# Attention on one core: VectorE sums four tiles of probabilities in one operation, and TensorE's 32-column sets go from six in four blocks to five in three

## The chip, the cores and the metric

The kernel runs on one core of one Trainium2 chip. The metric is the device time of one execution, in microseconds (us).

## What is computed

A gated cross-attention block and a gated feed-forward block. The part that matters here is the attention over 4 batches and 16 heads, with 1024 queries, 2048 keys and 32 columns a head:

```python
attn = jnp.einsum('bhqd,bhkd->bhqk', q, k) * scale
attn = jnp.clip(attn, -CLAMP, CLAMP)
attn = jax.nn.softmax(attn, axis=-1)
x = jnp.einsum('bhqk,bhkd->bqhd', attn, v).reshape(B, Nq, Cq)
```

Around it stand the projections of the queries, keys and values, the output projection, and the feed-forward network, which the change does not touch.

## The kernel before

The stages follow one another: `project_queries`, `project_keys_values`, `attend`, `project_out`, `feed_forward`. Only `attend` is changed.

**Units and steps.** A unit is one half of one head: 512 queries against all 2048 keys. There are 128 units. Each goes through four steps. In a step TensorE computes two different things in turn:

- `scores` (L683): for 128 queries of the unit that is being scored, one 512-key quarter into each of the PSUM banks 0 to 3. Quarters 0 and 1 are half 0, quarters 2 and 3 are half 1. VectorE reduces each half (128x1024) to one maximum a row, `maxima` (L868). The next step's scores of a half wait for this step's maximum of that half (`max_done`), since they overwrite its banks.
- `keys` (L702): for the unit whose maxima are known, the scores once more, transposed (128 keys by 512 queries), with the negated maximum folded in as two extra rows. ScalarE takes the exponential (`exps`, L806) into `probT`, sixteen tiles of 128x512 a unit. Three PSUM banks rotate under these, so a `keys` matmul waits for an earlier exponential.

The lags in the line `TURN, KEYS, PV, SUMS, FOLD = 5, 6, (9, 10), 11, 12` say how many steps behind its scoring a unit comes to each piece of work. I call a step by its number modulo 4: step 3 is the last of a unit's scoring. After its two maxima VectorE does `split_maxima`, five tiny reductions that combine and split the row maxima, at the end of step 3.

**What is summed.** A unit's 32-column work on TensorE goes to the four 32-partition groups of PSUM bank 7, one matmul a group; four (or three) such matmuls are a set. Four sets are the probabilities times the values (`values`, L741), two blocks of two sets. ScalarE copies bank 7 to `partial` (L827), and TensorE adds the four groups with `fold` (L752). The softmax denominators need the sum of all sixteen tiles. GpSimd adds the first twelve into `gp_sum` (L627, L632), and the column sums are matmuls with a tile of ones: tiles 12, 13 and 14 in `fold_values` (L754), tile 15 and the two halves of `gp_sum` in `last_sums` (L765). ScalarE then copies the result out of bank 7 (`gather`, L837).

**The order on TensorE in a step** is written out by hand: scores 0, keys 0, scores 1, keys 1, then whichever of `values`, `fold_values`, `last_sums` and `turn_maxima` (L723, which transposes the negated maxima; ScalarE copies them to `q_stack`, L818) belongs there, then scores 2, keys 2, scores 3, keys 3. Before the change there is one block in each step: `last_sums` in step 0, `values` and `turn_maxima` in step 1, `values` in step 2, `fold_values` in step 3.

VectorE's order in a step is maximum of half 0, maximum of half 1, and `split_maxima` in step 3. Every engine runs its own program in order; semaphores join them. A loop body holds 24 steps, six units.

## Time and profile before

| what | before |
|---|---|
| time, median of 3 runs | 3306.59 us (3306.49 to 3313.1) |
| the profiled execution's own time | 3304.32 us |
| its span | 3302.5 us |
| TensorE busy over the span | 3096.9 us (94%) |
| VectorE, ScalarE, GpSimd busy | 1998.2 (61%), 1558.6 (47%), 1911.2 (58%) us |
| mean granted TensorE clock | 0.969 |

The span is cut into stages by the first and last instruction of each. The attention stage runs from the first scores at 478.38 us to the last `gather` at 2344.47 us, more than half of the whole. In it the pattern of one unit repeats, so what one unit takes, times the number of units, is the stage.

### The profile page before, as it was taken

The page shows a single profiled execution, that of the slowest core. Times are in us where ns is not written, and L with a number is a line of the kernel's source. Part 1 is how long each engine was busy: PE and PEld are TensorE (multiplying, and loading weights), DVE is VectorE, ACT ScalarE, POOL GpSimd, SP SyncE. Part 2 cuts the span into 40 slices and gives each one's busy share as a digit, 9 for nine tenths or more (in the row PEclk, how much of TensorE's full clock was granted, in tenths as well). Part 3 has the DMA queues.
Part 4 walks back from the last instruction along what each step waited for, and adds up shares of the span by engine and source line. Part 5 has one row for each costly group of instructions (what it writes and reads, how often), then busy time and mean ns, then how long its engine had stood idle before and what let it go on. Part 6 is the DMA issues. An engine that isn't in the chain of part 4 may idle for free. (4 is left out here: it accounts for less than half of the span.)

```text
span 3302.5 us, 51612 instructions
## 1 busy us (share of the span) xinstructions
PE 3096.9 (94%) x15941; PEld 1905.8 (58%) x15941; DVE 1998.2 (61%) x2788; ACT 1558.6 (47%) x2847; POOL 1911.2 (58%) x897
## 2 busy tenths in 40 slices
PE   6799979999999999999999999999564999999999
PEld 5588854444444444444444444444243788888887
DVE  8766657666766666676666667666387333333332
ACT  2222217766766777676677667677321211111111
POOL 4655538888888888888888888888453100000000
PEclk9899979999999999999999999999777999999999
DMA  4556672222221222222122222211485000000000
GB/s 165 203 193 216 213 246 63 59 58 58 58 55 47 52 58 58 58 58 53 47 54 58 58 58 58 54 46 38 147 256 166 1 26 26 26 26 26 26 13 13
DMA packets 142094, 263.25 MB, mean 80 GB/s; under 512 B 16960, under 2 KB 57920, under 8 KB 134720
## 3 DMA queue, kind: packets, MB, share of 16 engines
q1 hardware_dynamic: 141344, 253.82, 27.1%
q10 hardware_dynamic: 672, 8.39, 0.8%
q8 instruction: 49, 0.80, 0.1%
q14 instruction: 29, 0.24, 0.0%
HBM read 168.84 MB, written 93.32 MB: 79 GB/s over the span
## 5 line engine op out<-in xcount | busy, mean ns | idle before, releaser
L868 DVE TENSOR_REDUCE at_half_max<-ps 128x1 f32<-128x1024 f32 x1024 | 1210.0, 1221 | 555.1 <-PE ps L683 548.2
L632 POOL TENSOR_TENSOR at_gp_sum<-at_gp_sum,at_probT 128x1024 f32<-128x1024 f32 x512 | 1218.6, 2380 | 42.1
L806 ACT ACTIVATE at_probT<-ps 128x512 f32<-128x512 f32 x2048 | 1071.1, 601 | 159.8 <-PE ps L702 139.0
L683 PE MATMUL ps<-at_k_stack,at_q_stack 96*128 96x512 f32 x2048 | 877.3, 430 | 27.2 <-DMA at_k_stack<-kT_hi 17.8
L702 PE MATMUL ps<-at_q_stack,at_k_stack 98*128 98x512 f32 x2048 | 808.2, 396 | 1.4 <-ACT at_probT L806 1.1
L683 PEld LDWEIGHTS ps<-at_k_stack,at_q_stack 96*128 96x128 f32 x2048 | 389.8, 191 | 465.5 <-DVE at_half_max L868 383.2
L741 PE MATMUL ps<-at_probT,at_v_head 128*32 128x512 f32 x4096 | 492.5, 598 | 0.9 <-ACT at_probT L806 0.9
L627 POOL TENSOR_TENSOR at_gp_sum<-at_probT 128x1024 f32<-128x1024 f32 x128 | 304.2, 2377 | 316.4 <-ACT at_probT L806 316.4
L702 PEld LDWEIGHTS ps<-at_q_stack,at_k_stack 98*128 98x128 f32 x2048 | 390.2, 191 | 70.1 <-ACT at_probT L806 7.1
L1392 POOL TENSOR_TENSOR ff_x_in<-ff_x_in,ff_b_half 128x2048 f32<-128x2048 f32 x8 | 36.8, 4604 | 601.5 <-DVE ff_x_in L1414 601.5
L1377 ACT ACTIVATE ff_y<-ps,ff_b_t 128x512 f32<-128x512 f32 x128 | 88.2, 689 | 612.9 <-PE ps L1340 612.9
L1431 DVE CAST ff_y_hi<-ff_y 128x512 fp32r<-128x512 f32 x128 | 61.5, 481 | 483.8 <-PE ps L1355 476.9
L741 PEld LDWEIGHTS ps<-at_probT,at_v_head 128*32 128x32 f32 x4096 | 106.8, 109 | 246.5 <-issue 197.6
L1340 PE MATMUL ps<-ff_h_hi,w_hi 128*128 128x512 f32 x512 | 202.8, 396 | 5.7 <-DVE ff_h_lo L1423 5.7
L1355 PE MATMUL ps<-w_hi,ff_y_hi 128*128 128x512 f32 x512 | 204.4, 399 | 0.0
L1340 PE MATMUL ps<-ff_h_hi,w_lo 128*128 128x512 f32 x512 | 202.7, 396 | 0.0
L1340 PE MATMUL ps<-ff_h_lo,w_hi 128*128 128x512 f32 x512 | 202.6, 396 | 0.0
L1355 PE MATMUL ps<-w_hi,ff_y_lo 128*128 128x512 f32 x512 | 201.5, 393 | 0.0
L1355 PE MATMUL ps<-w_lo,ff_y_hi 128*128 128x512 f32 x512 | 201.4, 393 | 0.0
L818 ACT ACTIVATE at_q_stack<-ps 2x512 fp32r<-2x512 f32 x128 | 75.0, 586 | 244.7 <-PE ps L723 244.7
L82 POOL TENSOR_TENSOR kv_square<-kv_k_hi 128x512 f32<-128x512 f32 x64 | 77.0, 1203 | 129.0 <-ACT kv_k_hi L453 124.5
L827 ACT COPY at_partial<-ps 128x512 f32<-128x512 f32 x128 | 75.1, 587 | 146.3 <-PE ps L741 146.3
(154 smaller groups left out, 3867.9 us busy)
## 6 DMA issues: line engine op xcount, KB each, us to landing
at_k_stack<-kT_hi SPq DMA_DIRECT2D x128, 256.0 KB, 4.9
kT_hi<-kv_k_hi SPq DMA_DIRECT2D x16, 1024.0 KB, 4.2
kT_lo<-kv_k_lo SPq DMA_DIRECT2D x16, 1024.0 KB, 6.5
v_heads<-kv_v_out SPq DMA_DIRECT2D x16, 1024.0 KB, 5.7
at_q_stack<-qT_hi SPq DMA_DIRECT2D x128, 128.0 KB, 3.3
at_k_stack<-kT_lo SPq DMA_DIRECT2D x64, 256.0 KB, 4.3
at_v_head<-v_heads SPq DMA_DIRECT2D x64, 256.0 KB, 5.1
kv_c_in<-in_ctx_dram SPq DMA_DIRECT2D x16, 768.0 KB, 7.2
```

The lines of the kernel that those rows point to most:

```text
L82: pool.tensor_tensor(square[:, :], tile, tile, ALU.mult).then_inc(bound_done, 1)
L627: pool.tensor_tensor(gp_sum[lane % 2][:, :, :], pairs[:, 0:2, :], pairs[:, 2:4, :], ALU.add) \
L632: pool.tensor_tensor(gp_sum[lane % 2][:, :, :], gp_sum[lane % 2][:, :, :], pairs[:, 2 * i + 2:2 * i + 4, :], ALU.add).then_inc(gp_added, 1)
L683: mm = pe.matmul(ps[:, n, :], q_stack[buf][0:PARTS, rows], k_stack[buf][0:PARTS, BANK * n:BANK * (n + 1)], start=True, stop=True)
L702: pe.matmul(ps[:, key_bank(lane, kv), :], k_stack[buf][0:rows, P * kv:P * (kv + 1)], q_stack[buf][0:rows, q:q + BANK], start=True, stop=Tr ...
L741: mm = pe.matmul(ps[D * g:D * (g + 1), 7, :], v_head[buf][:, 4 * r + g, :], probT[lane % 2][:, 4 * r + g, :], start=(r == 0), stop=(r == Q ...
L806: act.activation(probT[lane % 2][:, kv, :], src, ACT.Exp).then_inc(exp_done, 1)
L827: act.copy(partial[:, :], ps[:, 7, :]).then_inc(partial_done, 1)
L868: dve.tensor_reduce(dst, src, AX_X, ALU.max).then_inc(max_done, 1)
L1340: mm = pe.matmul(ps[:, 4 + f % 2, :], w1[a][:, kt, P * f:P * (f + 1)], b[:, kt, :], start=(n == 0), stop=(n == len(parts) - 1))
L1355: mm = pe.matmul(ps[:, t, :], a[f % 2][:, cols], w2[b][:, f, :], start=(f == 0 and n == 0), stop=(f == FT - 1 and n == 2))
L1377: act.activation(y[f % 2][:, :], ps[:, 4 + f % 2, :], ACT.Silu, bias=b1_t[:, f:f + 1]) \
```

## The change

`fold_values` and `last_sums` become one function, `fold`: one set of four matmuls, the fold of `partial`, a column sum of the new tile `rest_sum`, and the two column sums of `gp_sum`. `rest_sum` is written by VectorE, in a new function `add_rest`: one `tensor_reduce` over tiles 12 to 15 of `probT`, 4 x 512 elements a partition, summed over the four. Its access pattern reads the four tiles' same column one after the other, 2048 bytes apart. It stands at the end of VectorE's step, after the maxima. The two blocks of values move one step later (lags 10 and 11), `fold` stands at lag 13, and the copy to `partial` moves with the second block. VectorE also runs the few steps behind the last scores, for the last `add_rest`.

```diff
-    TURN, KEYS, PV, SUMS, FOLD = 5, 6, (9, 10), 11, 12
+    TURN, KEYS, FOLD = 5, 6, 13
+    PV = ((10, (0, 1)), (11, (2, 3)))
+    REST, REST_LAGS = 12, (10,)
...
-            def fold_values(base, slot):
-
-                unit, lane, r = unit_at(base, slot, SUMS)
+            def fold(base, slot):
+
+                unit, lane, r = unit_at(base, slot, FOLD)
                 if unit is None or r:
                     return
                 pe.wait_ge(partial_done, unit + 1)
+                pe.wait_ge(rest_done, len(REST_LAGS) * (unit + 1))
+                pe.wait_ge(gp_added, GP_ADDS * (unit + 1))
                 pe.matmul(ps[0:D, 7, :], A["fold"][:, :], partial[:, :], start=True, stop=True)
-                for g in range(1, 4):
-                    mm = pe.matmul(ps[D * g:D * (g + 1), 7, :], ones[:, :], probT[lane % 2][:, KVT - 5 + g, :],
-                                   start=True, stop=False)
-                mm.then_inc(partial_read, 1)
-
-            def last_sums(base, slot):
-                unit, lane, r = unit_at(base, slot, FOLD)
-                if unit is None or r:
-                    return
-                pe.wait_ge(gp_added, GP_ADDS * (unit + 1))
-                for g, tile in ((1, probT[lane % 2][:, KVT - 1, :]), (2, gp_sum[lane % 2][:, 0, :]),
-                                (3, gp_sum[lane % 2][:, 1, :])):
-                    mm = pe.matmul(ps[D * g:D * (g + 1), 7, :], ones[:, :], tile, start=False, stop=True)
+                for g, tile in ((1, rest_sum[:, :]), (2, gp_sum[lane % 2][:, 0, :]), (3, gp_sum[lane % 2][:, 1, :])):
+                    mm = pe.matmul(ps[D * g:D * (g + 1), 7, :], ones[:, :], tile, start=True, stop=True)
                 mm.then_inc(fold_done, 1)
...
-                values(base, slot, PV[0], (0, 1))
-                values(base, slot, PV[1], (2, 3))
-                fold_values(base, slot)
-                last_sums(base, slot)
+                for lag, rounds in PV:
+                    values(base, slot, lag, rounds)
+                fold(base, slot)
                 turn_maxima(base, slot)
...
-                unit, lane, r = unit_at(base, slot, PV[1])
+                unit, lane, r = unit_at(base, slot, PV[-1][0])
                 if unit is None or r:
                     return
                 act.wait_ge(pv_done, unit + 1)
-                need(act, partial_read, unit)
+                need(act, fold_done, unit)
                 act.copy(partial[:, :], ps[:, 7, :]).then_inc(partial_done, 1)
...
+            def add_rest(base, slot):
+
+                for i, lag in enumerate(REST_LAGS):
+                    unit, lane, r = unit_at(base, slot, lag)
+                    if unit is None or r:
+                        continue
+                    width = BANK // len(REST_LAGS)
+                    cols = slice(width * i, width * (i + 1))
+                    dve.wait_ge(exp_done, KVT * (unit + 1))
+
+                    need(dve, fold_done, unit)
+                    dve.tensor_reduce(rest_sum[:, cols], probT[lane % 2][:, REST:KVT, cols].rearrange("p t n -> p n t"),
+                                      AX_X, ALU.add).then_inc(rest_done, 1)
...
                 shift(base, slot, 3)
-
-            run_steps(dve, step, STEPS, UNROLL, first=1, tail=TAIL if clipping else 0)
+                add_rest(base, slot)
+
+            run_steps(dve, step, STEPS, UNROLL, first=1, tail=TAIL)
```

TensorE, in the steps behind the loop, where no register instructions stand between the matmuls. Before, from the set of `last_sums` in step 0 to the values and the transposed maxima in step 1:

```order
L765 MATMUL ps<-at_probT,at_ones 32x512
L765 MATMUL ps<-at_gp_sum,at_ones 32x512 x2
L683 MATMUL ps<-at_k_stack,at_q_stack 128x512
L702 MATMUL ps<-at_q_stack,at_k_stack 128x512
L683 MATMUL ps<-at_k_stack,at_q_stack 128x512
L702 MATMUL ps<-at_q_stack,at_k_stack 128x512
L683 MATMUL ps<-at_k_stack,at_q_stack 128x512
L702 MATMUL ps<-at_q_stack,at_k_stack 128x512
L683 MATMUL ps<-at_k_stack,at_q_stack 128x512
L702 MATMUL ps<-at_q_stack,at_k_stack 128x512
L741 MATMUL ps<-at_probT,at_v_head 32x512 x8
L723 MATMUL ps<-at_ident_r,at_neg_hi 2x128 x4
```

TensorE now, the same place: the last four matmuls of step 0, the first four of step 1, and its block (scores are now L687, keys L706):

```order
L687 MATMUL ps<-at_k_stack,at_q_stack 128x512
L706 MATMUL ps<-at_q_stack,at_k_stack 128x512
L687 MATMUL ps<-at_k_stack,at_q_stack 128x512
L706 MATMUL ps<-at_q_stack,at_k_stack 128x512
L687 MATMUL ps<-at_k_stack,at_q_stack 128x512
L706 MATMUL ps<-at_q_stack,at_k_stack 128x512
L687 MATMUL ps<-at_k_stack,at_q_stack 128x512
L706 MATMUL ps<-at_q_stack,at_k_stack 128x512
L758 MATMUL ps<-at_partial,fold 32x512
L760 MATMUL ps<-at_rest_sum,at_ones 32x512
L760 MATMUL ps<-at_gp_sum,at_ones 32x512 x2
L727 MATMUL ps<-at_ident_r,at_neg_hi 2x128 x4
```

Step 0 has lost its block: from the values of step 3 to the fold of step 1 TensorE has sixteen score and key matmuls and nothing between. Step 1 has the fold where it had two sets of values.

VectorE before, in the last two units of scoring: eight maxima, the five small reductions, and the next unit's maxima.

```order
L868 TENSOR_REDUCE at_half_max<-ps 128x1 x8
L893 TENSOR_REDUCE at_neg_pair<-at_half_max 128x4
L894 TENSOR_REDUCE at_neg_pair<-at_half_max 128x4
L896 TENSOR_REDUCE at_neg_hi<-at_half_max 128x4
L898 TENSOR_REDUCE at_neg_lo<-at_neg_pair 128x4
L900 TENSOR_REDUCE at_neg_hi<-at_neg_lo 128x4
L868 TENSOR_REDUCE at_half_max<-ps 128x1 x8
```

VectorE now, the same place (the maxima are L862, the new reduction L907, the small ones L887 to L894):

```order
L862 TENSOR_REDUCE at_half_max<-ps 128x1 x6
L907 TENSOR_REDUCE at_rest_sum<-at_probT 128x512
L862 TENSOR_REDUCE at_half_max<-ps 128x1 x2
L887 TENSOR_REDUCE at_neg_pair<-at_half_max 128x4
L888 TENSOR_REDUCE at_neg_pair<-at_half_max 128x4
L890 TENSOR_REDUCE at_neg_hi<-at_half_max 128x4
L892 TENSOR_REDUCE at_neg_lo<-at_neg_pair 128x4
L894 TENSOR_REDUCE at_neg_hi<-at_neg_lo 128x4
L862 TENSOR_REDUCE at_half_max<-ps 128x1 x6
```

The new reduction stands behind both maxima of step 2 and ahead of both maxima of step 3.

## Rows read from the trace of the kernel before

**Rows 1.** Windows, one unit: stretch, then busy of PE, PEld, DVE, ACT, POOL, clock, DMA, GB/s

```profile
1003.23:1017.60 14.37, 14.37 (x83) 7.00 (x83) 9.99 (x14) 10.10 (x20) 11.89 (x6) 1.00 0.25 59
```

**Rows 2.** One line, L752: all its matmuls over the whole span

```profile
L752 PE MATMUL ps<-at_partial,fold x256: 592/605/617, 512.5 to 2342.6; 128*32 128x512 f32 x128
```

**Rows 3.** Timeline of PE, steps 0 to 3 of one unit: start, length

```profile
1005.96 0.39 PE L702 MATMUL ps<-at_q_stack,at_k_stack 98*128 98x512 f32 x1
1006.28 0.62 PE L765 MATMUL ps<-at_probT,at_ones 128*32 128x512 f32 x1
...
1007.27 0.50 PE L683 MATMUL ps<-at_k_stack,at_q_stack 96*128 96x512 f32 x1
1007.61 0.40 PE L702 MATMUL ps<-at_q_stack,at_k_stack 98*128 98x512 f32 x1
...
1008.07 0.39 PE L702 MATMUL ps<-at_q_stack,at_k_stack 98*128 98x512 f32 x1
1008.44 0.50 PE L683 MATMUL ps<-at_k_stack,at_q_stack 96*128 96x512 f32 x1
...
1009.56 1.92 PE L741 MATMUL ps<-at_probT,at_v_head 128*32 128x512 f32 x16
1011.42 0.40 PE L723 MATMUL ps<-at_ident_r,at_neg_hi 128*2 128x128 f32 x4
1011.66 0.45 PE L683 MATMUL ps<-at_k_stack,at_q_stack 96*128 96x512 f32 x1
...
1012.65 0.40 PE L683 MATMUL ps<-at_k_stack,at_q_stack 96*128 96x512 f32 x1
...
1013.35 0.39 PE L702 MATMUL ps<-at_q_stack,at_k_stack 98*128 98x512 f32 x1
1013.67 1.92 PE L741 MATMUL ps<-at_probT,at_v_head 128*32 128x512 f32 x16
1015.53 0.50 PE L683 MATMUL ps<-at_k_stack,at_q_stack 96*128 96x512 f32 x1
...
1016.10 0.40 PE L683 MATMUL ps<-at_k_stack,at_q_stack 96*128 96x512 f32 x1
```

**Rows 4.** Timeline of DVE, the same unit

```profile
1005.23 1.22 DVE L868 TENSOR_REDUCE at_half_max<-ps 128x1 f32<-128x1024 f32 x1 [0.70 <-PE ps L683]
1006.58 0.16 DVE L893 TENSOR_REDUCE at_neg_pair<-at_half_max 128x4 f32<-128x8 f32 x1
...
1007.16 3.51 DVE L868 TENSOR_REDUCE at_half_max<-ps 128x1 f32<-128x1024 f32 x3
...
1016.54 2.36 DVE L868 TENSOR_REDUCE at_half_max<-ps 128x1 f32<-128x1024 f32 x2 [1.56 <-PE ps L683]
```

**Rows 5.** Timeline of PE and of DVE while the pipeline fills

```profile
502.30 0.39 PE L702 MATMUL ps<-at_q_stack,at_k_stack 98*128 98x512 f32 x1
503.28 0.50 PE L683 MATMUL ps<-at_k_stack,at_q_stack 96*128 96x512 f32 x1 [0.59 <-DVE at_half_max L868]
...
502.01 3.50 DVE L868 TENSOR_REDUCE at_half_max<-ps 128x1 f32<-128x1024 f32 x3
```

**Rows 6.** Timeline of ACT: the copy of the maxima in step 1

```profile
1011.86 0.59 ACT L818 ACTIVATE at_q_stack<-ps 2x512 fp32r<-2x512 f32 x1 [1.56 <-PE ps L723]
```

**Rows 7.** Groups over the span: count, busy us, mean ns, idle before

```profile
L868 DVE TENSOR_REDUCE at_half_max<-ps 128x1 f32<-128x1024 f32 x1024 | 1210.0, 1221 | 555.1 <-PE ps L683 548.2
...
L502 DVE TENSOR_REDUCE kv_ends<-q_sq_sum 128x1 f32<-128x512 f32 x1 | 0.7, 676 | 0.0
...
L487 DVE SCALAR_TENSOR_TENSOR not_finite<-kv_k_hi,not_finite 128x512 f32<-128x512 f32 x64 | 61.6, 963 | 0.0
...
L1414 DVE SCALAR_TENSOR_TENSOR ff_x_in<-ff_normed,ff_coef,ff_x_in 128x512 f32<-128x512 f32 x32 | 24.1, 752 | 1.1
...
L632 POOL TENSOR_TENSOR at_gp_sum<-at_gp_sum,at_probT 128x1024 f32<-128x1024 f32 x512 | 1218.6, 2380 | 42.1
...
L806 ACT ACTIVATE at_probT<-ps 128x512 f32<-128x512 f32 x2048 | 1071.1, 601 | 159.8 <-PE ps L702 139.0
```

More of the change, by code:

```diff
@@ L573, in attend @@
         neg_pair = sb("neg_pair", [P, QT, 2])
+        rest_sum = sb("rest_sum", [P, BANK])
         neg_lo = sb("neg_lo", [P, QT, 1])
@@ L602, in attend @@
         partial_done = sem("partial_done")
-        partial_read = sem("partial_read")
+        rest_done = sem("rest_done")
         fold_done = sem("fold_done")
```

## Prediction

> **What bounds the kernel now.** I read the windows of one unit first: in the 14.37 us from one unit's fold to the next, TensorE is busy for all 14.37, VectorE for 9.99, ScalarE for 10.10, GpSimd for 11.89, at full granted clock [rows 1]. The fold's matmuls run 128 units (two records each) from 512.5 to 2342.6 us, 14.4 us apart [rows 2]. So the attention stage is TensorE's queue. I then read the timeline of one unit, to see what is work in that queue and what is a wait.
>
> Between ordinary score and key matmuls the starts are 0.235 us apart (1012.65 to 1013.35 is three of them). A block costs more than its matmuls: the last key matmul before `last_sums` starts at 1005.96, the set at 1006.28, the next score matmul at 1007.27, the one behind it at 1007.61 [rows 3]. That is 1.65 us where two spacings would be 0.47, so a block of one set costs 1.18 us, of which 0.32 is the gap ahead of it, 0.99 the set, and 0.10 a longer first spacing.
>
> One spacing in the unit is a wait. Between 1008.07 and 1008.44 there are 0.37 us instead of 0.235. The score matmul at 1008.44 opens step 1 and overwrites half 0 of step 0. VectorE had started that half's maximum only at 1007.16, because it first had the maximum of half 1 of step 3 (started 1005.23) and then the five small reductions (from 1006.58) [rows 3, 4]. From the start of that half-1 maximum to the score matmul that opens step 1 it is 1008.44 - 1005.23 = 3.21 us, and nothing on TensorE shortens it. **I call this the split chain.** Today it is nearly hidden, because step 0 has a block that fills the time. Where it is not filled, the trace shows what it costs: while the pipeline fills, step 8 (a step 0) has no block yet, VectorE starts the maximum behind the small reductions at 502.01, and TensorE sits from its last start at 502.30 to 503.28, 0.98 us [rows 5].
>
> **The change part by part.** *TensorE's work.* One set and one block go: 1.18 us a unit. A turn or a copy is neither added nor removed. If TensorE went on without waits, the unit would take 14.37 - 1.18 = 13.2, and without today's wait of 0.13 about 13.1.
>
> *VectorE's work.* Added: one reduction of 2048 elements a partition. The trace has none of this form. A reduction of 1024 takes 1221 ns, one of 512 takes 676 [rows 7]: 1.064 ns an element and 0.13 us fixed, so 0.13 + 2048 x 1.064 = 2.31 us. Three maxima in a row take 3.51 us, 1.17 apart, 0.05 less than one alone [rows 4], so the next instruction comes 2.26 us behind. That is my value if the 2048-byte steps of the access pattern cost nothing; no row here has such steps. The upper end: GpSimd's adds, the slowest engine per element here, take 2380 ns for 1024 elements [rows 7], which would be 4.8 us for 2048; twice VectorE's time per element gives 4.5. The lower end is the reduction hidden entirely. VectorE's sum, about 10.0 + 2.3 = 12.3 us, is still under 13.1. The sum is not what decides; the place is.
>
> *The place.* The reduction stands ahead of step 3's maxima, and behind these comes the split chain, now beside a step 0 without a block. I follow one unit, with starts from the rows, zero at the score matmul that opens step 1:
>
> - to the block 1.12 (1008.44 to 1009.56); the set 0.99; the transposed maxima 0.24 (1011.42 to 1011.66); to the score matmul that opens step 2, 0.99 (1011.66 to 1012.65): together 3.34;
> - in step 2 three spacings, 0.70, to the second key matmul. It needs the exponential of tile 14. ScalarE now has two copies ahead of it in step 1: the maxima's begins 0.44 behind its matmul (1011.42, 1011.86 [rows 3, 6]), at 2.11 + 0.44 = 2.55; it and the result's copy take about 0.57 each one behind the other, the exponential 0.60 [rows 7], which ends at 4.29. The matmul would start at 4.04: a new wait of 0.25, and the spacing behind a pause is 0.10 longer. Then the gap 0.32 and two sets, 1.86 (1013.67 to 1015.53), the second score matmul of half 1, 0.57 later (1016.10), and 0.44 to VectorE (1016.54 [rows 4]). Together 3.34 + 0.70 + 0.35 + 0.32 + 1.86 + 0.57 + 0.44 = 7.58 us, when the maximum of half 1 of step 2 starts;
> - from there VectorE has no pause: that maximum 1.17, the new reduction 2.26, the maximum of half 0 of step 3 1.17, then the split chain 3.21, at whose end TensorE opens the next step 1. Together 7.81 us.
>
> The unit takes 7.58 + 7.81 = **15.39 us**, 1.02 more than 14.37. Saved matmuls are in it already; TensorE would wait about 2.1 to 2.3 us a unit. Times about 126 units in the steady pattern (the first and last are fill and drain) this is +128 us; I take +127, since fill differs. At the end of the stage nothing changes: the last `last_sums` waited for GpSimd's last add, and `fold` does too. The other stages are untouched. The profiled execution took 3304.3 us, the median of the runs is 3306.6, 2.3 more; 3304.3 + 127 = 3431, by the median 3434. **I predict 3432 us.**
>
> *If the reduction were free.* From the start of step 1, TensorE reaches half 1 of step 3 at 7.58 + 0.47 + 0.70 + 0.32 + 1.86 + 0.57 = 11.50 us, then comes the split chain, 3.21: 14.71, still 0.34 more than before, +43 us. So moving the blocks costs by itself, since step 0 has lost its filler, and the reduction counts in full once it is over 3.92 - 1.17 - 1.17 = 1.58 us.
>
> **A rule against the change.** No row here shows a reduction from SBUF with far steps. The Trainium skill, "Advanced Engine Details and Errata", section on SBUF cachelines, says that ScalarE and VectorE want at least two hits on a 16-byte line and pay a penalty when each access goes to another line; this pattern does so at every element. It gives no figure for VectorE.
>
> **The rivals.** (1) *The strided read is slow.* Every element of the pattern lies 2048 bytes from the one before. Per-element time doubled gives 4.49 us, 2.18 more a unit on the same path: 17.57 us, +403 us, 3708. Half more gives 16.48 us and 3571. Nothing in the trace speaks for or against. This is the result that the page's rule would have here.
>
> (2) *VectorE and GpSimd hinder each other.* A two-input VectorE operation beside GpSimd's squares takes 963 ns (L487), one of the same size in the feed-forward stage 752 (L1414) [rows 7]. By that factor, 1.28, the reduction takes 2.96 us: 16.04 us a unit, 3515. Against it: it has one input. The Trainium skill, "SBUF - State Buffer", section on who interferes with whom, says that a `tensor_reduce` never contends with GpSimd on trn2. By that this rival is nothing; no reduction beside GpSimd from SBUF stands in the trace but tiny ones.
>
> (3) *TensorE stays the bound: faster.* The unit takes 13.1 us, 1.27 less, times 126: -160 us, 3147. It needs the split chain to be under 3.21 - (14.71 - 13.1) = 1.6 us even with a free reduction. For it: TensorE is busy all the time now, and VectorE's sum fits. Against it: rows 5 and 4 show the chain at its length, and the wait at 1008.44 shows that it binds already.
>
> (4) *The reduction mostly hides*, since it needs less time than I think or part of VectorE's work finds slack: toward 14.71 us, 3350. The trace's only reduction rates speak against it.
>
> That the change does nothing measurable would need the unit within 0.05 us of 14.37, which no case gives.
>
> **How the numbers follow.** Forecast (3390 to 3480): 0.60. Rival 1 (3480 to 3715): 0.25. Rival 2 (near 3515): 0.05. Rival 4 (3340 to 3390): 0.05. Rival 3: 0.04. No change: 0.01. A change of 0.2%, about 6.6 us, is about what a measurement of this kernel can tell. Faster 0.04, same 0.01, slower 0.95. The forecast's own range is 3390 to 3480: the ScalarE wait may be absent (-0.35 us a unit, -44) or the reduction a few tenths longer (+0.3 gives +38). The range for all takes in the doubled read, since leaving rival 1 out would leave over 2 in 10: 3385 to 3715.
>
> **What the changed profile would show.** The fold's matmuls 15.4 us apart, not 14.4. The group of the new reduction: 128 of about 2.3 us; its mean decides between the forecast and rivals 1, 2 and 4. TensorE's score matmul waiting for VectorE by about 1 us or more where step 1 opens, and less where step 0 opens; TensorE's busy share in a unit down to about 85%. VectorE without a pause from step 2's second maximum to step 1. A key matmul in step 2 waiting about 0.25 us for ScalarE. GpSimd's adds unchanged at 2380 ns. The prediction is wrong if the split chain shortens when VectorE is saturated (in rows 5 the queue looks a little tighter than in the loop), or if the new reduction's length is not 2.3 us.

## The result: slower by a sixth

The changed kernel takes 3846.05 us (median of 4 runs, 3840.93 to 3848.53), the kernel before 3306.61 us in the same comparison: ratio 1.1624, 95% interval 1.1604 to 1.1644. The forecast's direction was right. Its time, 3432, was 414 us too low, and its range ended at 3715.

The page of the changed kernel, busy times by engine and two groups (count, busy us, mean ns, idle before):

```profile
PE 3367.2 (88%) x15173; PEld 2064.9 (54%) x15173; DVE 2491.5 (65%) x2916; ACT 1595.2 (41%) x2847; POOL 1901.9 (49%) x897
...
L687 PE MATMUL ps<-at_k_stack,at_q_stack 96*128 96x512 f32 x2048 | 1039.8, 509 | 295.7 <-DVE at_half_max L862 275.0
...
L907 DVE TENSOR_REDUCE at_rest_sum<-at_probT 128x512 f32<-128x2048 f32 x128 | 494.7, 3865 | 11.6 <-ACT at_probT L800 11.6
```

Two things stand there that the prediction did not have. The new reduction takes 3865 ns, not 2310. And the score matmuls (L687) have a mean of 509 ns, where the page of the kernel before has 430, although nothing about them was changed.

The matmuls of `fold`, first and last start, give the length of a unit: (2885.8 - 524.6) / 127 = 18.59 us, where [rows 2] give 14.41.

```profile
L758 PE MATMUL ps<-at_partial,fold x256: 590/1061/1062, 524.6 to 2885.8; 128*32 128x512 f32 x128
```

TensorE's timeline in one unit, from the end of step 3 to the set in step 1:

```profile
1209.66 0.40 PE L706 MATMUL ps<-at_q_stack,at_k_stack 98*128 98x512 f32 x1
1212.13 0.79 PE L687 MATMUL ps<-at_k_stack,at_q_stack 96*128 96x512 f32 x1 [2.07 <-DVE at_half_max L862]
1212.72 0.63 PE L706 MATMUL ps<-at_q_stack,at_k_stack 98*128 98x512 f32 x1
1213.15 0.63 PE L687 MATMUL ps<-at_k_stack,at_q_stack 96*128 96x512 f32 x1
...
1217.55 1.06 PE L758 MATMUL ps<-at_partial,fold 128*32 128x512 f32 x1
```

VectorE's timeline beside it:

```profile
1205.94 1.23 DVE L862 TENSOR_REDUCE at_half_max<-ps 128x1 f32<-128x1024 f32 x1 [1.55 <-PE ps L687]
1207.08 3.87 DVE L907 TENSOR_REDUCE at_rest_sum<-at_probT 128x512 f32<-128x2048 f32 x1
1210.85 2.36 DVE L862 TENSOR_REDUCE at_half_max<-ps 128x1 f32<-128x1024 f32 x2
1213.34 0.16 DVE L887 TENSOR_REDUCE at_neg_pair<-at_half_max 128x4 f32<-128x8 f32 x1
...
1213.92 1.22 DVE L862 TENSOR_REDUCE at_half_max<-ps 128x1 f32<-128x1024 f32 x1
```

The order is the predicted one: half 1 of step 2 at 1205.94, the reduction, step 3's two maxima, the small reductions, half 0 of step 0. TensorE opens step 0 at 1212.13 after 2.07 us of waiting. From there its matmuls start 0.43 us apart, where [rows 3] have 0.235: the engine runs at its lower clock. In the unit before, and in every second one from 1000 to 1300 us, the first four behind the same wait still start at full-clock spacing, and the fall comes about 1.5 us after the wait's end:

```profile
1193.26 0.50 PE L687 MATMUL ps<-at_k_stack,at_q_stack 96*128 96x512 f32 x1 [2.06 <-DVE at_half_max L862]
1193.60 0.39 PE L706 MATMUL ps<-at_q_stack,at_k_stack 98*128 98x512 f32 x1
1193.83 0.40 PE L687 MATMUL ps<-at_k_stack,at_q_stack 96*128 96x512 f32 x1
...
1195.05 0.63 PE L687 MATMUL ps<-at_k_stack,at_q_stack 96*128 96x512 f32 x1
1195.48 0.63 PE L706 MATMUL ps<-at_q_stack,at_k_stack 98*128 98x512 f32 x1
```

Windows of that trace (length, then busy of PE, PEld, DVE, ACT, POOL, then the granted clock):

```profile
1190.80:1193.26 2.46, 0.40 (x2) 0.00 (x1) 2.46 (x3) 1.04 (x2) 2.38 (x2) 1.00 0.00 0
...
1197.77:1201.50 3.73, 3.73 (x16) 1.35 (x15) 1.22 (x1) 1.67 (x4) 2.36 (x1) 0.50 0.00 0
1202.00:1209.66 7.66, 7.66 (x48) 3.55 (x48) 6.08 (x4) 4.67 (x11) 2.71 (x2) 1.00 0.65 154
1212.13:1217.00 4.87, 4.87 (x12) 3.80 (x12) 4.07 (x8) 2.59 (x5) 4.00 (x2) 0.50 0.00 0
```

The first window is the idle time in the unit before. Once a unit the clock goes to 0.50 (1.2 GHz), and it is back at 1.00 (2.4 GHz) ahead of the two blocks of values. From 700 to 2100 us its mean is 0.82; in the kernel before it is 1.00.

### The profile page after: what moved, and what is told of

Read it like the earlier page. It is cut to its first block and busy times, and to the rows that moved or that the text cites. A ratio compares the mean times of both kernels' runs of the same rounds, so it can differ in the third digit from the quotient of the medians.

```text
span 3846.7 us, 50579 instructions
## 1 busy us (share of the span) xinstructions
PE 3367.2 (88%) x15173; PEld 2064.9 (54%) x15173; DVE 2491.5 (65%) x2916; ACT 1595.2 (41%) x2847; POOL 1901.9 (49%) x897
## 5 line engine op out<-in xcount | busy, mean ns | idle before, releaser
L862 DVE TENSOR_REDUCE at_half_max<-ps 128x1 f32<-128x1024 f32 x1024 | 1221.7, 1219 | 622.3 <-PE ps L687 615.1
L800 ACT ACTIVATE at_probT<-ps 128x512 f32<-128x512 f32 x2048 | 1119.5, 602 | 707.2 <-PE ps L706 698.5
L687 PE MATMUL ps<-at_k_stack,at_q_stack 96*128 96x512 f32 x2048 | 1039.8, 509 | 295.7 <-DVE at_half_max L862 275.0
L636 POOL TENSOR_TENSOR at_gp_sum<-at_gp_sum,at_probT 128x1024 f32<-128x1024 f32 x512 | 1210.0, 2363 | 90.4 <-ACT at_probT L800 53.2
L706 PE MATMUL ps<-at_q_stack,at_k_stack 98*128 98x512 f32 x2048 | 972.5, 475 | 6.4 <-ACT at_probT L800 1.1
L687 PEld LDWEIGHTS ps<-at_k_stack,at_q_stack 96*128 96x128 f32 x2048 | 473.0, 232 | 729.7 <-DVE at_half_max L862 493.6
L706 PEld LDWEIGHTS ps<-at_q_stack,at_k_stack 98*128 98x128 f32 x2048 | 483.2, 236 | 126.7 <-ACT at_probT L800 41.1
L907 DVE TENSOR_REDUCE at_rest_sum<-at_probT 128x512 f32<-128x2048 f32 x128 | 494.7, 3865 | 11.6 <-ACT at_probT L800 11.6
L758 PE MATMUL ps<-at_partial,fold 128*32 128x512 f32 x256 | 223.3, 975 | 0.9 <-DVE at_rest_sum L907 0.9
L760 PE MATMUL ps<-at_gp_sum,at_ones 128*32 128x512 f32 x512 | 223.6, 973 | 0.0
L760 PE MATMUL ps<-at_rest_sum,at_ones 128*32 128x512 f32 x256 | 223.1, 975 | 0.0
```

Of the source, the lines that this page charges most:

```text
L636: pool.tensor_tensor(gp_sum[lane % 2][:, :, :], gp_sum[lane % 2][:, :, :], pairs[:, 2 * i + 2:2 * i + 4, :], ALU.add).then_inc(gp_added, 1)
L687: mm = pe.matmul(ps[:, n, :], q_stack[buf][0:PARTS, rows], k_stack[buf][0:PARTS, BANK * n:BANK * (n + 1)], start=True, stop=True)
L706: pe.matmul(ps[:, key_bank(lane, kv), :], k_stack[buf][0:rows, P * kv:P * (kv + 1)], q_stack[buf][0:rows, q:q + BANK], start=True, stop=Tr ...
L758: pe.matmul(ps[0:D, 7, :], A["fold"][:, :], partial[:, :], start=True, stop=True)
L760: mm = pe.matmul(ps[D * g:D * (g + 1), 7, :], ones[:, :], tile, start=True, stop=True)
L800: act.activation(probT[lane % 2][:, kv, :], src, ACT.Exp).then_inc(exp_done, 1)
```

## The experiments

I held two theories of the 540 us. **A**: the new reduction is long because of its far steps. It stands ahead of the split chain, so it counts in full: 15.39 + (3.87 - 2.31) = 16.95 us a unit by the prediction's own walk. **B**: the rest, 18.59 - 16.95 = 1.64 us a unit, is the lower clock that TensorE gets after its long wait. The rivals were that short groups or GpSimd make the reduction long, that VectorE's sum of work is what counts, and that the clock costs nothing. Lengths of a unit below are worked out as above, from the first and last start of the fold's matmuls.

**Near elements** (`e1_near`). The same amount of reduction, without far steps.

```diff
-                    dve.tensor_reduce(rest_sum[:, cols], probT[lane % 2][:, REST:KVT, cols].rearrange("p t n -> p n t"),
-                                      AX_X, ALU.add).then_inc(rest_done, 1)
+                    dve.tensor_reduce(rest_sum[:, cols], probT[lane % 2][:, REST:KVT, cols].rearrange("p t n -> p (t n)")
+                                      .rearrange("p (n t) -> p n t", t=KVT - REST), AX_X, ALU.add).then_inc(rest_done, 1)
```

> The changed kernel, but the reduction reads four neighbouring elements for each sum (the same 2048 elements, the same 512 sums, no far steps). It leaves out the right pairing, so the sums are of other elements. Theory A (the 2048-byte steps make the reduction long): the reduction falls from 3.87 us to about 2.3, a unit to about 15.4 us, the time to about 3430 us. Theory B (512 short groups of four make it long, whatever the steps): the reduction stays at 3.87 us and the time at 3846 us.

3421.5 us, ratio 1.0336 (1.0319 to 1.0353). The reduction by itself, shortest, median and longest ns:

```profile
L907 DVE TENSOR_REDUCE at_rest_sum<-at_probT x128: 2274/2276/2286, 514.8 to 2456.2; 128x512 f32<-128x2048 f32 x128
```

Theory A holds: the groups are as short, GpSimd is as busy, and only the far steps are gone. It took 2.28 us, 0.03 from the prediction's 2.31, and the time is 10 us from its 3432. The unit took 15.27 us, where the walk gave 15.39. TensorE now waits in two places, where step 0 and where step 1 open. Five units in six have waits as in the first two lines; in the sixth the second wait is as in the last line:

```profile
1194.23 0.50 PE L687 MATMUL ps<-at_k_stack,at_q_stack 96*128 96x512 f32 x1 [0.48 <-DVE at_half_max L862]
1197.29 0.50 PE L687 MATMUL ps<-at_k_stack,at_q_stack 96*128 96x512 f32 x1 [0.72 <-DVE at_half_max L862]
...
1212.99 0.50 PE L687 MATMUL ps<-at_k_stack,at_q_stack 96*128 96x512 f32 x1 [1.13 <-DVE at_half_max L862]
```

From 700 to 2100 us no wait for a maximum is longer than these, and the clock is 1.00 in every window of 2 us.

**No reduction** (`e2_no_reduce`). TensorE's order alone.

```diff
-                pe.wait_ge(rest_done, len(REST_LAGS) * (unit + 1))
...
-                for g, tile in ((1, rest_sum[:, :]), (2, gp_sum[lane % 2][:, 0, :]), (3, gp_sum[lane % 2][:, 1, :])):
+                for g, tile in ((1, probT[lane % 2][:, KVT - 1, :]), (2, gp_sum[lane % 2][:, 0, :]), (3, gp_sum[lane % 2][:, 1, :])):
...
-                add_rest(base, slot)
-
-            run_steps(dve, step, STEPS, UNROLL, first=1, tail=TAIL)
+
+            run_steps(dve, step, STEPS, UNROLL, first=1, tail=TAIL if clipping else 0)
```

> The changed kernel without the reduction on VectorE: TensorE's order stays as changed, and fold takes tile 15 in place of the sum of tiles 12 to 15, so tiles 12 to 14 are left out of the denominators. Split-chain theory (moving the blocks costs by itself, since step 0 has no filler): 14.7 us a unit, about 3350 us, slower than before. Rival (TensorE stays the bound, and all of the loss is the reduction): 13.1 us a unit, about 3150 us.

3355.77 us, ratio 1.0142 (1.0125 to 1.0159); 14.73 us a unit, where the prediction's walk had 14.71 for a free reduction. So moving the blocks costs by itself, though it takes a set of matmuls away. The waits of this kernel from 700 to 2100 us (us in total, times, longest) show TensorE on the split chain, once in each of the 94 units or so:

```profile
PE ps L687 <- DVE at_half_max L861: 74.3, 94, 1.1
```

**Filler** (`e3_filler`). The reduction keeps its length; TensorE gets useless work where it waits.

```diff
+                for _ in range(7 if kv == 7 else 0):
+                    pe.matmul(ps[:, key_bank(lane, kv), :],
+                              k_stack[buf][0:rows, P * kv:P * (kv + 1)], q_stack[buf][0:rows, q:q + BANK],
+                              start=True, stop=True)
                 pe.matmul(ps[:, key_bank(lane, kv), :],
```

> The changed kernel with seven more matmuls a unit that do the same key tile again, where TensorE now sits idle for 2.06 us (end of step 3). Clock theory (that idle time lets TensorE's granted clock fall to half, and this costs about 1.7 us a unit beyond the longer reduction): the clock stays near full, a unit takes about 16.9 us, the time falls to about 3620 us although work is added. Rival (the clock costs nothing, the unit is bound by VectorE's path alone): 3846 us or a little more.

3632.08 us, ratio 1.0977 (1.0959 to 1.0995): with 896 more matmuls the kernel is 214 us faster than the changed one. The unit took 16.92 us, where theory A alone gives 16.95. TensorE's timeline (step 2, then the end of step 3) and the window from 700 to 2100 us:

```profile
1204.44 0.39 PE L687 MATMUL ps<-at_k_stack,at_q_stack 96*128 96x512 f32 x1
1204.93 0.50 PE L710 MATMUL ps<-at_q_stack,at_k_stack 98*128 98x512 f32 x1
...
1211.95 1.78 PE L707 MATMUL ps<-at_q_stack,at_k_stack 98*128 98x512 f32 x7
1213.57 0.39 PE L710 MATMUL ps<-at_q_stack,at_k_stack 98*128 98x512 f32 x1
1214.46 0.50 PE L687 MATMUL ps<-at_k_stack,at_q_stack 96*128 96x512 f32 x1 [0.51 <-DVE at_half_max L866]
...
700.00:2100.00 1400.00, 1288.66 (x6821) 666.27 (x6817) 1129.16 (x1150) 841.54 (x1560) 980.85 (x412) 1.00 0.19 47
```

The wait of 2.07 us has become 0.51, a second one, where step 1 opens, is about 0.7 us (1.14 in one unit of six). The mean clock from 700 to 2100 us is 1.00: in these 1400 us it falls to 0.50 three times, each time behind a wait of the longer kind. Nothing on VectorE was changed. So theory B holds too. By the unit lengths the clock's share is (18.59 - 16.92) x 127 = 212 us.

**The reduction added to the kernel before** (`e4_add_only`). Blocks as before, sums as before, `add_rest` in addition, its result unused.

```diff
                 pe.wait_ge(gp_added, GP_ADDS * (unit + 1))
+                pe.wait_ge(rest_done, unit + 1)
...
                 shift(base, slot, 3)
+                add_rest(base, slot)
```

> The kernel before, with the new reduction added at the same place in VectorE's order and its result unused; TensorE's blocks stay in all four steps. Path theory (the reduction at 3.87 us stands ahead of the split chain and counts in full): 8.10 us on TensorE to the maximum of half 1 of step 2, then 1.17 + 3.82 + 1.17 + 3.21: 17.5 us a unit, about 3700 us at full clock, more if the clock falls. Rival (the filler in step 0 hides most of it, so the loss is the block order's): under 3450 us.

4067.18 us, ratio 1.2292 (1.2271 to 1.2312): 20.36 us a unit. The filler of step 0 doesn't hide the reduction. The walk's 17.5 us is at full clock; here TensorE waits up to 3.0 us for a maximum and the mean clock is 0.83. One unit of the trace, from the opening of step 0 at 1215.45 to the next at 1235.99 (20.54 us), shows where the time above the walk lies:

```profile
1215.45 0.50 PE L686 MATMUL ps<-at_k_stack,at_q_stack 96*128 96x512 f32 x1 [2.93 <-DVE at_half_max L872]
...
1221.59 3.12 PE L744 MATMUL ps<-at_probT,at_v_head 128*32 128x512 f32 x16
...
1229.79 1.22 DVE L872 TENSOR_REDUCE at_half_max<-ps 128x1 f32<-128x1024 f32 x1 [1.57 <-PE ps L686]
```

From 1229.79, the maximum of half 1 of step 2, to 1235.99 it is 6.20 us, and the walk has 1.17 + 3.82 + 1.17 = 6.16. From 1215.45 to 1229.79 it is 14.34, where the walk has 3.21 + 8.10 = 11.3. In that stretch TensorE waits for nothing, but the clock is 0.54 from 1217.90 to 1224.60, and the block of values takes 3.12 us where [rows 3] have 1.92. So the time above the walk stands where the clock is low. No run held the clock up here.

**The reduction between the maxima** (`f1_between`).

```diff
                 shift(base, slot, 1)
+                add_rest(base, slot)
                 if s is not None:
                     maxima(slot, s, 1)
...
                 shift(base, slot, 3)
-                add_rest(base, slot)
```

> The changed kernel with the reduction moved on VectorE from the end of step 2 to between the two maxima of step 2, where VectorE waits for TensorE's block of values anyway. Place theory (only what delays step 3's maxima and the split chain counts): about 2 us of the 3.87 is hidden, a unit takes about 15.0 us, 3385 us, and the clock stays full since TensorE's longest wait falls under 2 us. Rival (VectorE's sum of work is what counts, wherever it stands): unchanged, 3846 us.

3382.63 us, ratio 1.0226 (1.0209 to 1.0243); 14.97 us a unit. One line of VectorE's order moved gives back 463 us: VectorE waits for half 1 of step 2 anyway, since its scores stand behind the block of values. The wait is what hides it: against the version without the reduction, e2_no_reduce, it costs 27 us here, and 490 at the end of the step. Part of the 463 is the clock's, since against e3_filler, where the clock was held up, the move brings 249. The longest wait of TensorE for a maximum is down to 1.1 us, with a mean clock of 0.99. The expectation that the clock stays full was not quite right: behind 8 of the 15 waits of 1.1 us in the 1400 us it still fell to 0.50 for some 3 us, as here:

```profile
1196.91 0.66 PE L687 MATMUL ps<-at_k_stack,at_q_stack 96*128 96x512 f32 x1 [1.12 <-DVE at_half_max L862]
1197.37 0.63 PE L706 MATMUL ps<-at_q_stack,at_k_stack 98*128 98x512 f32 x1
1197.80 0.63 PE L687 MATMUL ps<-at_k_stack,at_q_stack 96*128 96x512 f32 x1
```

**The set in step 0** (`f2_fold12`).

```diff
-    TURN, KEYS, FOLD = 5, 6, 13
+    TURN, KEYS, FOLD = 5, 6, 12
```

> The changed kernel with fold one step earlier (lag 12, step 0), so that the set stands where the split chain runs and step 1 holds only the transposed maxima; the reduction stays at the end of step 2. Filler theory: 1.1 us of the chain is covered again, a unit takes about 15.8 us at full clock, 3485 us, more if TensorE's wait ahead of step 0 still lets the clock fall. Rival (the place of the set is indifferent, one block is one block): 3846 us.

3756.07 us, ratio 1.1351 (1.1332 to 1.137); 17.95 us a unit, 0.64 less than the changed kernel. The clock still falls (mean 0.85, longest wait 2.1 us), so the full-clock figure can't be read from it.

**Both moves** (`f3_both`): the two edits above together.

> Both moves: reduction between the maxima of step 2, fold in step 0. By the two theories together a unit takes about 14.1 us, 3265 us, faster than the kernel before although the reduction keeps its 3.87 us. Rival (the reduction's length alone decides, since it exceeds the idle time of 1.6 to 2 us in its place): over 3306 us.

3242.95 us, ratio 0.9801 (0.9785 to 0.9818); 13.92 us a unit. With the same reduction of 3.87 us and the same five sets in three blocks, the kernel is 2.0% faster than the one before and 603 us faster than the changed one. Against f1_between only the set's place differs, and both clocks are near full: 140 us, or 1.05 us a unit, which is what f2_fold12 could not show by itself. VectorE has hardly a pause now:

```profile
1201.55 5.98 DVE L862 TENSOR_REDUCE at_half_max<-ps 128x1 f32<-128x1024 f32 x5
1207.45 3.90 DVE L907 TENSOR_REDUCE at_rest_sum<-at_probT 128x512 f32<-128x2048 f32 x1
1211.28 3.50 DVE L862 TENSOR_REDUCE at_half_max<-ps 128x1 f32<-128x1024 f32 x3
```

**Two additions in place of the reduction** (`f4_adds`), with both moves. The intermediate sum lies in `clipped`, which the path taken here doesn't use.

```diff
-                    dve.tensor_reduce(rest_sum[:, cols], probT[lane % 2][:, REST:KVT, cols].rearrange("p t n -> p n t"),
-                                      AX_X, ALU.add).then_inc(rest_done, 1)
...
+                dve.tensor_tensor(pair, last[:, 0:2, :], last[:, 2:4, :], ALU.add).then_inc(pair_done, 1)
+                dve.wait_ge(pair_done, unit + 1)
+                need(dve, fold_done, unit)
+                dve.tensor_tensor(rest_sum[:, :], pair[:, 0, :], pair[:, 1, :], ALU.add).then_inc(rest_done, 1)
```

> As both moves, but the four tiles are summed by two ordinary additions of neighbouring elements (1024, then 512 elements a partition) in place of the reduction. At 1.2 + 0.7 us, or up to 1.3 times that beside GpSimd, they hide wholly: a unit takes about 13.4 us, 3190 us, and TensorE is nearly the bound again. Rival (two-input additions and GpSimd's adds block one another): the additions take 3 us or more or GpSimd's get longer, over 3265 us.

3359.14 us, ratio 1.0154 (1.0137 to 1.0171), 116 us slower than with the slow reduction. Shortest, median and longest of each addition:

```profile
L908 DVE TENSOR_TENSOR at_clipped<-at_probT x128: 1212/2598/3037, 511.4 to 2389.0; 128x1024 f32<-128x1024 f32 x128
L911 DVE TENSOR_TENSOR at_rest_sum<-at_clipped x128: 691/693/2839, 512.6 to 2391.7; 128x512 f32<-128x512 f32 x128
```

The rival is right here. The first addition takes 1.21 us at best and 2.60 in the median, the second up to 2.84, which is its own 0.69 and most of one of GpSimd's 2.38; GpSimd's adds take up to 3.17. This is what rival 2 of the prediction feared of the reduction, and what the reduction does not do: 2274 to 2286 ns in all 128 of the near ones, beside the same GpSimd. The Trainium skill, "SBUF — State Buffer", section on who interferes with whom, has it so: two inputs from SBUF contend with GpSimd's reads, a `tensor_reduce` never does. The traces agree with both halves.

**Distances** (`f5_steps`). Eleven operations behind the last unit, one line each:

```diff
+            dve.wait_ge(fold_done, UNITS)
+            dve.tensor_reduce(flat, four.rearrange("p (n t) -> p n t", t=4), AX_X, ALU.add).then_inc(bench, 1)
+            dve.tensor_reduce(flat.rearrange("p (a b) -> p a b", b=2),
+                              four.rearrange("p (a t b) -> p a b t", t=4, b=2), AX_X, ALU.add).then_inc(bench, 1)
...
```

> The changed kernel with eleven more VectorE operations behind the last attention unit, when GpSimd is done: seven reductions of 2048 elements in groups of four, with 1, 2, 4, 8, 16, 128 and 512 elements (of 4 bytes) between the elements of a group; then groups of two and of eight at 512 elements' distance (1024 and 4096 elements), one reduction of all 2048 to one sum, and an addition of 512. Line theory (a 16-byte line read once costs more): 2.28 us at distances 1 and perhaps 2, 3.87 us from 4 elements on, the same whatever the distance beyond; by element the long ones cost 1.82 ns, so groups of eight take about 7.6 us and groups of two 2.0 us. Rival (a cost that grows with the distance, or belongs to each group rather than each element): a slope over 8, 16, 128, 512, or 0.8 us for 512 groups whatever their size.

One run, 3879.85 us; only the durations are read. L946 to L963 read groups of four whose elements lie 1, 2, 4, 8, 16, 128 and 512 elements (of 4 bytes) apart; L965 is groups of two and L967 groups of eight at 512, and L969 sums 2048 neighbours to one:

```profile
2886.81 2.29 DVE L946 TENSOR_REDUCE at_rest_sum<-at_probT 128x512 f32<-128x2048 f32 x1 [1.23 <-PE ps L761]
2889.13 2.29 DVE L948 TENSOR_REDUCE at_rest_sum<-at_probT 128x512 f32<-128x2048 f32 x1
2891.45 3.77 DVE L951 TENSOR_REDUCE at_rest_sum<-at_probT 128x512 f32<-128x2048 f32 x1
2895.26 3.77 DVE L954 TENSOR_REDUCE at_rest_sum<-at_probT 128x512 f32<-128x2048 f32 x1
2899.07 3.57 DVE L957 TENSOR_REDUCE at_rest_sum<-at_probT 128x512 f32<-128x2048 f32 x1
2902.67 3.62 DVE L960 TENSOR_REDUCE at_rest_sum<-at_probT 128x512 f32<-128x2048 f32 x1
2906.33 3.62 DVE L963 TENSOR_REDUCE at_rest_sum<-at_probT 128x512 f32<-128x2048 f32 x1
2909.98 1.23 DVE L965 TENSOR_REDUCE at_rest_sum<-at_probT 128x512 f32<-128x1024 f32 x1
2911.24 7.03 DVE L967 TENSOR_REDUCE at_rest_sum<-at_probT 128x512 f32<-128x4096 f32 x1
2918.31 2.29 DVE L969 TENSOR_REDUCE at_rest_sum<-at_probT 128x1 f32<-128x2048 f32 x1
```

One group of 2048 takes as long as 512 groups of four (2.29 us), so the number of groups costs nothing that shows. The step comes between 8 bytes (2.29 us) and 16 bytes (3.77), and beyond 16 the distance hardly matters. That is the Trainium skill's rule ("SBUF — State Buffer", the note on cachelines: full bandwidth wants two hits on a 16-byte line), and the trace agrees for groups of four and eight. It does not for groups of two: there, too, each element lies 2048 bytes from the one before, and 1024 of them take 1.23 us, no more than the 1.22 of a maximum over 1024 neighbours (in PSUM). My expectation of 2.0 us for them was wrong. L963 is the pattern of the changed kernel and takes 3.62 us here, with GpSimd and TensorE idle, and 3.87 in the loop; the near reduction takes the same in both places (2.29, 2.28). No run tells what the 0.25 us in the loop come from.

**Near elements with both moves** (`f7_both_near`): the first edit on top of both moves.

> Both moves and the reduction on neighbouring elements (wrong pairing, so other sums): the reduction takes 2.28 us beside GpSimd. If the reduction's length is all that still binds the version with both moves, the unit takes 13.4 us, 3185 us; if TensorE's order or ScalarE binds it already, it stays at 3243 us.

3204.91 us, ratio 0.9688 (0.9672 to 0.9704); 13.59 us a unit. It is between the two: the reduction's far steps still cost 38 us in the version with both moves, and 20 us less than expected come back.

**Interleaved tiles** (`f6_interleaved`). Both moves and the right sums with near reads: tiles 12 to 15 lie interleaved, for the exponentials, the values and the reduction.

```diff
+    def tile_of(pairs, kv):
+        if kv < REST:
+            return pairs[:, kv, :]
+        return pairs[:, REST:KVT, :].rearrange("p t n -> p (t n)").rearrange("p (n t) -> p n t", t=KVT - REST)[:, :, kv - REST]
...
-                                       probT[lane % 2][:, 4 * r + g, :], start=(r == 0), stop=(r == QT - 1))
+                                       tile_of(probT[lane % 2], 4 * r + g), start=(r == 0), stop=(r == QT - 1))
...
-                act.activation(probT[lane % 2][:, kv, :], src, ACT.Exp).then_inc(exp_done, 1)
+                act.activation(tile_of(probT[lane % 2], kv), src, ACT.Exp).then_inc(exp_done, 1)
```

> As the kernel before it, but with the right sums: tiles 12 to 15 lie interleaved in memory, so ScalarE writes them and TensorE reads them with 16 bytes between elements, and VectorE reads neighbours. If far steps cost VectorE's reads only: 3185 us. If they also cost TensorE's moving reads or ScalarE's writes about 0.8 ns an element: 4 matmuls in one set and 4 exponentials a unit longer by 0.4 us or more each, 3240 us or above.

3546.21 us, ratio 1.0716 (1.0694 to 1.0738): 303 us slower than the far reads on VectorE, and 341 slower than `f7_both_near`, from which it differs only in where the four tiles lie. Groups of it, 700 to 2100 us:

```profile
L806 ACT ACTIVATE at_probT<-ps 128x512 f32<-128x512 f32 x1374 | 873.2, 735 | 155.3 <-PE ps L712 141.8
...
L751 PE MATMUL ps<-at_probT,at_v_head 128*32 128x512 f32 x2752 | 436.6, 757 | 0.0
```

The exponentials' mean rises from 601 to 735 ns, and TensorE's values matmuls' from 598 to 757. From 1200 to 1230 us, where the clock is 1.00, single ones reach 1159 and 1079 ns. The 16 bytes between elements cost on both, not on VectorE alone.

**Sums of pairs** (`f8_pairs`), with both moves.

```diff
-                    dve.tensor_reduce(rest_sum[:, cols], probT[lane % 2][:, REST:KVT, cols].rearrange("p t n -> p n t"),
-                                      AX_X, ALU.add).then_inc(rest_done, 1)
+                for i in range(2):
+                    two = probT[lane % 2][:, REST + 2 * i:REST + 2 * i + 2, :].rearrange("p t n -> p n t")
+                    dve.tensor_reduce(pair[:, i, :], two, AX_X, ALU.add).then_inc(pair_done, 1)
+                dve.wait_ge(pair_done, 2 * unit + 2)
+                dve.tensor_reduce(rest_sum[:, :], pair.rearrange("p t n -> p n t"), AX_X, ALU.add).then_inc(rest_done, 1)
```

> Both moves, and the sum of four tiles made of three reductions over groups of two (tiles 12 and 13, 14 and 15, then the two sums) one behind the other, each reading two tiles 2048 bytes apart. Groups of two took 1.23 us in the run of distances, no more than neighbours. Two-line theory (only groups that walk over more than two far places are slow): each takes 1.23 us also beside GpSimd, 3.6 us together, 0.2 us less than the one of 3.87, and the unit falls from 13.92 to about 13.7 us: about 3215 us. Rival (pairs are fast only when GpSimd is idle, or three operations cost more between them than they save): 3243 us or more.

3225.81 us, ratio 0.9749 (0.9736 to 0.9763); 13.76 us a unit. The reductions over pairs keep their length beside GpSimd:

```profile
L909 DVE TENSOR_REDUCE at_clipped<-at_probT x256: 1225/1242/1274, 510.2 to 2259.6; 128x512 f32<-128x1024 f32 x128
L912 DVE TENSOR_REDUCE at_rest_sum<-at_clipped x128: 1245/1255/1282, 512.6 to 2260.9; 128x512 f32<-128x1024 f32 x128
```

This is the best kernel with the reference's sums: 2.5% faster than the kernel before, 620 us faster than the changed one.

## Why the prediction was right or wrong

**The bound and the split chain: right.** TensorE's queue bounds the kernel before, and the chain from the maximum of half 1 of step 3 to the opening of step 1 becomes the bound where step 0 has no block. The version without the reduction took 14.73 us a unit for the 14.71 worked out. The parts that the prediction gives of a block's 1.18 us (0.32, 0.99 and 0.10) add up to 1.41, since the gap of 0.32 has one ordinary spacing of 0.235 in it; the walk uses the starts themselves, and so this changes nothing in it.

**The walk: right at its own lengths.** With a reduction of 2.28 us the unit took 15.27 (15.39 worked out) and the kernel 3421.5 us (3432). With 3.87 us and the clock held up it took 16.92 (16.95).

**The length of the reduction: the term that was mis-sized.** "0.13 + 2048 x 1.064 = 2.31 us. ... That is my value if the 2048-byte steps of the access pattern cost nothing." They cost 1.56 us. Rival 1, with a chance of 0.25, was the case that came, at a price between its "half more" (3.4 us) and "doubled" (4.49). By the walk it makes 1.56 x 126 = +197 us, 3629, inside the range.

**The step that failed: the walk's spacings at full clock.** The prediction took each spacing on TensorE from [rows 3], where the granted clock is 1.00, and put a wait of over 2 us into the same queue, saying that "TensorE would wait about 2.1 to 2.3 us a unit". It did not ask what such a wait does to the matmuls behind it. They started 0.43 us apart instead of 0.235, at once or 1.5 us after the wait, until the clock came back. That is 212 us, and it is what put the time outside the range. In the forecast's own case the assumption was sound: with the reduction at 2.28 us the waits for a maximum are 0.47 and 0.72 us (1.13 in one unit of six), and the clock did not fall. It failed in rival 1's case, whose 3571 and 3708 are at full clock too: the longer reduction put 2.07 us in one place, ahead of step 0.

The sum: 3306.6 before; moving the blocks 49 (no reduction); the reduction at near reads 66 (to 3421.5); its far steps 211 (to the filler's 3632.1); the clock 214. Together 3846.

**The other rivals.** Rival 2 (GpSimd and the reduction hinder each other) is ruled out for near reads by 2274 to 2286 ns in every one of them; of the far reads' 3.87 us at most the 0.25 that they take more in the loop than alone could be its. Rival 3 (TensorE stays the bound) and rival 4 (the reduction mostly hides) are false for this order. With the reduction in VectorE's wait rival 4's mechanism is real (f1_between, 27 us), and with both moves the unit goes part of the way to rival 3's 13.1 us: 13.92, and 13.59 with near reads. Of the page's rule behind rival 1: the prediction has it for ScalarE and VectorE, while the section of the Trainium skill that it cites names no engine, and f6_interleaved shows the cost on TensorE's reads as well. The new wait of a key matmul for ScalarE came at its size: in e3_filler the second key matmul of step 2 starts 0.49 us behind the score matmul ahead of it (1204.44, 1204.93), 0.25 more than the 0.235 of [rows 3]; the profile does not name what it waited for.

**Signs named ahead.** The new group's mean was named as what decides between the cases, and it did. "GpSimd's adds unchanged" was right (2363 ns). TensorE's wait "by about 1 us or more where step 1 opens, and less where step 0 opens" was right at 2.28 us (0.72 and 0.47) and the wrong way round at 3.87: 2.07 where step 0 opens, 0.2 or nothing where step 1 does. TensorE's busy share was to be 85%; it was 88% from 700 to 2100 us, and 91% with the reduction at 2.28 us.

What stays open: what e4_add_only would take with the clock held up, where the 0.25 us of the far reads in the loop come from, and why groups of two are spared the cost of far steps.

## What to carry to other kernels

Where work is taken off the busiest engine, ask which waits that work was covering: here one set of matmuls hid a chain of VectorE work, and taking it away cost more than it saved until another set stood there. Added work on a second engine goes where that engine already waits, not at the end of its step; the same instruction cost 490 us in one place, the lower clock that came of it included, and 27 in the other. And a long wait on TensorE may be paid twice: look at the granted clock of the matmuls behind it, and if it falls, price the stretch at the lower clock.

## What the runs showed of the hardware

- VectorE's reduction from SBUF in groups of four: 2.29 us for 2048 elements when the elements of a group lie 4 or 8 bytes apart, 3.57 to 3.77 from 16 bytes to 2048 (f5_steps), and 3.87 at 2048 bytes in the loop. Groups of two 2048 bytes apart: 1.23 us for 1024 elements, and 1.24 beside GpSimd (f8_pairs).
- Where the four tiles lay interleaved (f6_interleaved), ScalarE's exponential, writing every 16 bytes, took up to 1159 ns (601 in the mean before), and TensorE's 32-column fp32 matmul, whose moving elements lie 16 bytes apart, up to 1079 ns at full clock (598).
- In the kernels where TensorE waited 2.0 us or more once a unit, the granted clock went to 0.50 for the matmuls behind it (mean 0.82 to 0.85 from 700 to 2100 us); in those whose longest such wait was 1.1 us the mean was 0.99 or 1.00, and with two additions, where one unit in three waited 2.1 us, 0.96. A long wait was not all that came ahead of a fall: behind waits of 1.1 us the clock fell 8 times in 15 in f1_between, 3 times in all in e3_filler and never in e1_near, and in f6_interleaved it fell 16 times in the same 1400 us, though no wait of TensorE that its trace names was over 0.4 us.
- A VectorE addition of two SBUF tiles waited for GpSimd's running add, up to 2.84 us for one of 0.69 (f4_adds); reductions of near elements did not (2274 to 2286 ns in e1_near).
